# A megakernel on one core: FFN weights split in natural layout and turned by DMA, row terms joined behind the norm

## What is computed

```python
q1 = fake_quant(layernorm(x)); q2 = fake_quant(ctx)          # clip(round(x/s + z), 0, 255)
x = x + q1 @ q2
h = layernorm(x)
wg, wu, wd = block_qdq_weight(w_gate), ...                    # blocks of 32 along the input, 4 bits:
#   scale = max(|w|)/7 ;  wq = clip(round(w / scale), -8, 7) * scale
xq = act_qdq(h)                                               # 16 bits, one scale from min and max over all of h
up = act_qdq(xq @ wu.T); gate = act_qdq(xq @ wg.T)
gate = act_qdq(gate * fixed_qdq(sigmoid(gate)))
x = x + act_qdq(gate * up) @ wd.T
```

## Time and profile before

| | |
|---|---|
| median of three runs | 829.89 us |
| the profiled execution | 830.54 us |
| its span | 828.5 us |
| PE busy | 728.5 (88%) |
| DVE busy | 643.6 (78%) |
| ACT busy | 513.9 (62%) |
| POOL busy | 511.3 (62%) |
| mean granted TensorE clock | 0.954 |

### The profile page before, as it was taken

How to read it: one execution, slowest core, us unless ns; L and a number is a source line. 1 busy time by engine, 2 the same in 40 slices (tenths; PEclk the granted TensorE clock), 3 DMA queues, 4 the chain that set the end, 5 groups by cost and what they waited for, 6 DMA issues and landing times.

```text
span 828.5 us, 13514 instructions
## 1 busy us (share of the span) xinstructions
PE 728.5 (88%) x3443; PEld 342.7 (41%) x3443; DVE 643.6 (78%) x1374; ACT 513.9 (62%) x968; POOL 511.3 (62%) x488
## 2 busy tenths in 40 slices
PE   0688999736695996999999999999999788999998
PEld 0234545313232452444444444444444253444443
DVE  6885667678799678888888888888888767656655
ACT  4656766556857436777777777777776643655540
POOL 1986675546566557778888888888884414344330
PEclk9999999976888898999999999999999999999998
DMA  7211232201225326788666666666655512332311
GB/s 320 89 65 39 65 101 67 62 26 51 39 51 95 121 70 133 178 191 180 124 146 144 144 144 145 142 146 144 152 102 102 102 39 80 107 110 84 114 38 51
DMA packets 164500, 89.08 MB, mean 108 GB/s; under 512 B 154081, under 2 KB 154337, under 8 KB 161522
## 3 DMA queue, kind: packets, MB, share of 16 engines
q1 hardware_dynamic: 164466, 88.67, 42.9%
HBM read 49.85 MB, written 1.05 MB: 61 GB/s over the span
## 4 chain that ended last, share of the span: by engine, by line
PE 60%; DVE 13%; POOL 12%; issue 9%; DMA 2%; ACT 2%; SPq 1%; DVEq 0%; POOLq 0%; ACTq 0%
PE ps L950 19%; PE ps L951 19%; PE ps L952 19%; POOL arena L464 4%; POOL arena L472 3%; DVE arena L1290 3%; DVE arena L1293 2%; PE ps L1138 1%; POOL arena L604 1%; DMA arena<-arena 1%; DVE arena L1287 1%; POOL arena L451 1%; ACT arena L647 1%; POOL arena L482 1%; DVE ss L1449 1%
## 5 line engine op out<-in xcount | busy, mean ns | idle before, releaser
L950 PE MATMUL ps<-arena 128*128 128x512 f16 (+2 forms) x996 | 385.9, 388 | 25.7 <-DVE arena L1293 11.8
L951 PE MATMUL ps<-arena 128*128 128x512 f16 (+2 forms) x996 | 384.6, 386 | 0.0
L952 PE MATMUL ps<-arena 128*128 128x512 f16 (+2 forms) x996 | 384.2, 386 | 0.0
L647 ACT ACTIVATE arena<-arena 128x512 f16<-128x512 f32 (+9 forms) x392 | 260.8, 692 | 98.1 <-POOL arena L604 29.6
L1293 DVE SCALAR_TENSOR_TENSOR arena<-ps,arena 128x512 f32<-128x512 f32 (+2 forms) x182 | 122.9, 702 | 53.4 <-ACT arena L647 45.9
L950 PEld LDWEIGHTS ps<-arena 128*128 128x128 f16 (+1 forms) x996 | 99.5, 100 | 148.2 <-issue 34.6
L952 PEld LDWEIGHTS ps<-arena 128*128 128x128 f16 (+1 forms) x996 | 99.5, 100 | 122.6 <-issue 11.3
L951 PEld LDWEIGHTS ps<-arena 128*128 128x128 f16 (+1 forms) x996 | 99.5, 100 | 111.7 <-issue 9.2
L604 POOL TENSOR_SCALAR arena<-arena,rden 128x512 f32<-128x512 f32 x128 | 114.9, 898 | 25.3 <-DVE rden L1639 16.1
L1287 DVE TENSOR_TENSOR arena<-arena 128x512 f16<-128x512 f32 (+2 forms) x146 | 108.7, 779 | 5.3 <-ACT arena L647 4.8
L846 ACT ACTIVATE arena<-arena,mneg 128x512 f32<-128x512 f32 x124 | 88.5, 715 | 36.8 <-DVE mneg L1619 36.8
(11 more groups left out here) (126 smaller groups left out, 702.4 us busy)
## 6 DMA issues: line engine op xcount, KB each, us to landing
arena<-in_moe_w SPq DMA_DIRECT2D x18, 768.0 KB, 4.4
arena<-in_ffn_w SPq DMA_DIRECT2D x33, 256.0 KB, 2.7
arena<-in_wq SPq DMA_DIRECT2D x8, 1024.0 KB, 5.3
arena<-in_wo SPq DMA_DIRECT2D x8, 1024.0 KB, 5.3
arena<-in_kv_w SPq DMA_DIRECT2D x4, 1024.0 KB, 5.1
arena<-arena SPq DMA_TRANSPOSE x144, 3.3
arena<-in_ctx SPq DMA_DIRECT2D x1, 2048.0 KB, 9.5
arena<-in_ctx_t SPq DMA_DIRECT2D x1, 2048.0 KB, 13.9
```

The lines of the kernel that those rows point to most:

```text
L647: return a.activation(out_, in_, ACT.Copy, scale=scale, bias=bias)
L950: pe.matmul(out_, lhs[0], rhs[0], start=first, stop=False)
L951: pe.matmul(out_, lhs[0], rhs[1], start=False, stop=False)
L952: return pe.matmul(out_, lhs[1], rhs[0], start=False, stop=last)
```

## The change

It does four things.

1. The weights are no longer turned by PE. `scale_back` writes into one of four slots `deq`; ACT writes the high half from there (not from PSUM) and the low half is a subtraction of two SBUF tensors, on POOL for even chunks (`low`) and on DVE for odd ones (`weight_low`), both into `wt`, in natural layout. `turn_w(n)` on SP is a DMA transfer that transposes both halves (128x1024 f16) into `wfx`, where tile n reads them. `deq` and `wt` lie where `kt`, the turned K, comes later, so `turn_k(0)` waits until all turns have landed.
2. The chunks' parts run one or two chunks further ahead: ACT's high n + 2, POOL's low n + 2, scale_back n + 3, divide n + 4; DVE's maxima n + 5. All V units use banks 2 and 3. DVE's loops over chunks are unrolled.
3. In the first stage rounding is done by writing int32, which takes passes away: x from 3 to 2, ctx from 4 half passes to 2, the quantisation of `xn` from 3 flat passes to 2 for each row tile.
4. The row terms (`rsum`) are a constant for each row, which the norm removes, so the statistics no longer wait for them; ACT adds them after the extrema. The transposes of q1 are copied out earlier in ACT's order, `rstd(1)` stands between `kw_low(0, 1)` and `kw_low(0, 2)`, `spread(0)` after three V units and the transposes of the hidden after six.

```diff
+        wfx = carve(104, (WS, 2 * D), F16)
+        wf = [wfx[:, :, 0:D], wfx[:, :, D:2 * D]]
+        wt = carve(56, (DQ, 2 * D), F16)
+        deq = carve(64, (DQ, D))
...
+            def turn_w(n):
+                sp.wait_ge(w_lo[n % 2], n // 2 + 1)
+                if n >= WS:
+                    sp.wait_ge(f_ps, n - WS + 1)
+                sp.dma_start_transpose(wfx[:, n % WS].rearrange("p (a b) -> p a b", b=P),
+                                       wt[:, n % DQ]).then_inc(w_tr[n % DQ], 16)
...
+            for n in range(2, NCH):
+                turn_w(n)
+                if n + RAW + 1 < NCH:
+                    ring(n + RAW + 1)
+                if n == FT + 1:
+                    kw_load(3)
...
-                if n >= 2:
-                    g.wait_ge(w_t, n - 1)
-                g.tensor_tensor(deq[n % 2].rearrange("p (a b) -> p a b", b=QB), v, s, ALU.mult).then_inc(w_deq, 1)
+                if n >= DQ:
+                    g.wait_ge(w_lo[n % 2], (n - DQ) // 2 + 1)
+                g.tensor_tensor(deq[:, n % DQ].rearrange("p (a b) -> p a b", b=QB), v, s, ALU.mult).then_inc(w_deq, 1)
+
+            def low(n):
+                g.wait_ge(w_hi, n + 1)
+                g.tensor_tensor(wt[:, n % DQ, D:2 * D], deq[:, n % DQ], wt[:, n % DQ, 0:D], ALU.subtract)\
+                    .then_inc(w_lo[0], 1)
 
             def weights(n):
-                scale_back(n)
-                if n + 2 < NCH:
-                    divide(n + 2)
+                if n % 2 == 0 and n + 2 < NCH:
+                    low(n + 2)
+                if n + 3 < NCH:
+                    scale_back(n + 3)
+                if n + 4 < NCH:
+                    divide(n + 4)
...
-            for k in range(KD):
-                kw_low(0, k)
+            kw_low(0, 0)
+            kw_low(0, 1)
             rstd(1)
+            kw_low(0, 2)
+            kw_low(0, 3)
...
+            scale_back(0)
             kw_low(1, 2)
             kw_low(1, 3)
             v_low(3)
-            scale_back(0)
-            for u in range(4, MT - 1):
-                v_low(u)
-            g.wait_ge(xt_ps, KD)
             scale_back(1)
+            v_low(4)
+            v_low(5)
+            low(0)
+            v_low(6)
+            scale_back(2)
...
-                a.activation(half, half, ACT.Identity, bias=par[:, 3:4], scale=pc[:, 1:2]).then_inc(ctx_scaled, 1)
+                a.activation(ctx_int[:, b * KD:(b + 1) * KD], half, ACT.Relu, bias=par[:, 3:4],
+                             scale=pc[:, 1:2]).then_inc(ctx_scaled, 1)
...
-            a.wait_ge(row_terms, 1)
-            for t in range(NT):
-                a.wait_ge(col_added, t + 1)
+
+            def row_terms_in(t):
+
+                a.wait_ge(ext_ready, 1)
...
+            def weight_high(n):
+                a.wait_ge(w_deq, n + 1)
+                if n >= DQ:
+                    a.wait_ge(w_tr[n % DQ], 16 * (n // DQ))
+                copy(wt[:, n % DQ, 0:D], deq[:, n % DQ]).then_inc(w_hi, 1)
...
+            v_out(3)
+            for t in range(NT):
+                row_terms_in(t)
+            v_out(4)
+            weight_high(0)
+            v_out(5)
             hidden_high(0, 1.0)
+            weight_high(1)
+            v_out(6)
...
-                weight_high(n + 1)
+                weight_high(n + 2)
...
-                if i < FT - 1:
-                    weight_high(2 * FT + i + 1)
+                if i < FT - 2:
+                    weight_high(2 * FT + i + 2)
...
-                pe.wait_ge(w_lo, n + 1)
+                pe.wait_ge(w_tr[n % DQ], 16 * (n // DQ + 1))
...
-            for u in range(4):
+            for u in range(3):
                 v_unit(u)
             spread(0)
-            for u in range(4, MT - 1):
+            for u in range(3, 6):
                 v_unit(u)
             hidden_transposes(0)
-            v_unit(MT - 1)
-            pe.wait_ge(xt_lo, 1)
+            for u in range(6, MT):
+                v_unit(u)
             v_unit(MT)
...
-                stt(one(wf[1], n % WS), bank(2 + n % 2), SW, one(wf[0], n % WS), ALU.mult, ALU.subtract).then_inc(w_lo, 1)
+                tt(wt[:, n % DQ, D:2 * D], deq[:, n % DQ], wt[:, n % DQ, 0:D], ALU.subtract).then_inc(w_lo[1], 1)
...
-            own.link(ts(flat(xn), flat(xn), par[:, 2:3], ALU.add, MAGIC, ALU.add))
-            own.link(ts(flat(xn), flat(xn), MAGIC, ALU.max, MAGIC + 255.0, ALU.min))
-            ts(flat(q1), flat(xn), MAGIC + 128.0, ALU.subtract).then_inc(q1_ready, 1)
+            own.link(ts(flat(xn_int), flat(xn), par[:, 2:3], ALU.add, 0.0, ALU.max))
+            ts(flat(q1), flat(xn_int), 255.0, ALU.min, 128.0, ALU.subtract).then_inc(q1_ready, 1)
             for b in range(B):
-                half = flat(ctx_raw[:, b * KD:(b + 1) * KD])
                 v.wait_ge(ctx_scaled, b + 1)
-                own.mark(ts(half, half, MAGIC, ALU.add, MAGIC, ALU.max))
-            own.wait(own.n)
-            for b in range(B):
-                half = flat(ctx_raw[:, b * KD:(b + 1) * KD])
-                ts(flat(q2[:, b * KD:(b + 1) * KD]), half, MAGIC + 255.0, ALU.min, MAGIC + 128.0, ALU.subtract)\
-                    .then_inc(q2_ready, 1)
+                ts(flat(q2[:, b * KD:(b + 1) * KD]), flat(ctx_int[:, b * KD:(b + 1) * KD]), 255.0, ALU.min, 128.0,
+                   ALU.subtract).then_inc(q2_ready, 1)
...
-                v.wait_ge(row_added, t + 1)
+                v.wait_ge(col_added, t + 1)
...
-            own.link(ts(flat(xn), flat(xn), aqp[:, 0, 0:1], ALU.mult, MAGIC, ALU.add))
-            own.link(clip(flat(xn), 0))
-            ts(flat(xn), flat(xn), MAGIC, ALU.subtract, SINT, ALU.mult).then_inc(xn_ready, 1)
+            for t in range(NT):
+
+                own.link(ts(xn_int[:, t], xn[:, t], aqp[:, 0, 0:1], ALU.mult, aqp[:, 0, 2:3], ALU.min))
+                ts(xn[:, t], xn_int[:, t], SINT, ALU.mult).then_inc(xn_ready, 1)
...
-                m = block_maxima(n + 3)
-                weight_low(n)
-                m = scales(n + 3, m)
+                if n + 5 < NCH:
+                    m = block_maxima(n + 5)
+                if n % 2 and n + 2 < NCH:
+                    weight_low(n + 2)
+                if n + 5 < NCH:
+                    m = scales(n + 5, m)
                 if between:
                     between()
-                inverse_scales(n + 3, m)
+                if n + 5 < NCH:
+                    inverse_scales(n + 5, m)
```

More of the change, by code:

```diff
@@ L524, in _ @@
             divide(3)
-            weights(2)
+            weights(0)
             for k in range(KD):
@@ L558, in _ @@
                         k_low(u - 1)
-            for u in range(3, 2 * MT):
+            for u in range(4, 2 * MT):
                 k_pow(u)
@@ L1507, in _ @@
                 gate_front(i)
-            weights(2 * FT + 1)
+            for i in range(2):
+                weights(2 * FT + i)
             for i in range(2, FT):
```

152 lines of the change are left out of this document (62 added, 90 removed).

## The result

The changed kernel takes 833.49 us (median of five runs, 832.66 to 834.59) against 829.62 before in the same comparison: a ratio of 1.0054, 95% interval 1.003 to 1.0077. It is 0.5% slower, within the 1% that was called no change, and outside the 810 to 829 of the forecast. The profiled execution took 832.66 with a span of 830.8.

What follows compares the result with a forecast made beforehand. Bound by a cross-engine chain in the first stage, PE in the up tiles, the chunks' ring in late gate tiles, ACT and DVE in K. -18.3 to the third extrema, +7.5 in K: -10.8, so 819.5 us; range 810 to 829.

Steps and rivals of the forecast that it cites:

- the transfers' price: 33 new chunk transfers, each 3.1 to landing, hidden where PE sets the pace and costed at nothing.
- the ring of the last gate tiles: Last four gate tiles: a loop over ACT, POOL, DVE and PE, 5.9 per chunk before, is cut.
- the stall before `turn_k(0)`: K phase: ACT stands still while turn_k(0) waits for turn_w(32) to land; +7.5, bounds 0 and +9.
- Rival B: K phase: the stall at turn_k(0) is hidden or short; 812 us, 808 to 815; chance 0.20.
- D: DVE and POOL shut each other out of SBUF, the chunk's chain grows to 5.3; 845 us; chance 0.10.
- its eight passes of 0.54 end before 53.3: First stage: DVE's quantisation of the hidden per row tile starts at 48.0 and ends before 53.3.
- end by 43.4: First stage: PE's V0 to V2, at 2.6 each, end by 43.4, before the extrema are there.
- C: Gains lost in part, by the granted clock or a first stage still bound by POOL; 824 to 829; chance 0.20.
- what ACT has for it, 3.1 to 3.3: Gate tiles: a tile without V costs ACT's weight_high, rounding, copy and kw_high; five tiles taken at 3.3.
- 1.4 of loss until tile 5: Up tiles: tiles 2 and 4 wait for POOL's chunk parts; tile 5 at 82.8 against 90.83.
- I take 8.0: Up tiles: per pair PE 7.77, ACT 7.65, POOL 7.75; taken as 8.0, since they don't interlock exactly.
- I take no gain: K phase: ACT's wait on PE, 2.0 per pair, becomes a wait on DVE; no gain, bound -10.

Runs made afterwards that it cites:

- experiments 3 and 4: The changed kernel with the hidden quantised by two flat passes, 829.01 us; the changed kernel with POOL held until the hidden is quantised, 832.15 us (one run).
- experiment 6: The changed kernel with 40 added matmuls that keep PE busy ahead of V0; 831.3 us, ratio 1.0033 to the kernel before.
- experiment 7: The changed kernel with chunk 2's parts earlier in the orders of ACT and POOL; 831.8 us, ratio 1.0035 to the kernel before.
- experiment 5: The changed kernel with DVE's odd low halves one step later in the gating; 830.08 us, ratio 1.002 to the kernel before.

## Why the prediction was wrong

**What held.** The first extrema (44.5 forecast, 43.2), V0's start (35.6, 35.03), the transfers' price (3.1 to landing, 33 of them), the ring of the last gate tiles that is cut (5.9 apart before, 3.6 to 3.9 now), and the K phase: the stall before `turn_k(0)` was forecast with its place, its cause and 7.5 us, and it was 6.73 of wait; the stage is 7.3 longer. Rival B, that it would be hidden, is out. So is D at its price of 845, but not its mechanism: of the sixteen low halves on DVE five took 1.23 to 1.42, which was a sign of being wrong, and eleven 0.67 to 0.86.

The stages were forecast at 62.9, 44.0, 46.8 and 62.1 and took 67.9, 45.4, 52.0 and 62.0. Two terms failed, each by 5: the first stage and the gate tiles.

**The first stage, -9.4 forecast and -4.5 measured.** The step that failed most is the sentence "its eight passes of 0.54 end before 53.3". I had the rule of the ports in hand as rival D, with `rsum` as its row, and applied it only to the new subtractions, not to the eight short instructions that the same change makes of three long ones. They took 10.2 us instead of 4.3, as experiments 3 and 4 show. The right price was in the earlier trace rows: the flat pass took 1.96 beside POOL where the earlier trace rows has 1.22 for the form, 0.7 each; eight times that is the miss. Between V5's end and V6's start 4.9 passed instead of the 1.8 forecast; that is 3.1 of the 5.0 by which the first tile is late.

The other 2.0 are in V0 to V2, which should "end by 43.4" and ended at 45.7, behind the extrema. I used 2.6 per unit, the full-clock row, behind 10 us in which PE was idle; the drop of the clock stood among my rivals (C), but for the last gate tiles and not here. Worth 2.2 by the median of experiment 6.

**The gate tiles, 46.8 forecast and 52.0 measured.** I priced a tile without V by "what ACT has for it, 3.1 to 3.3" and left DVE out. The last ones came 3.6 to 3.9 apart, and DVE is busy 37.35 of the last 37.60 us; in 126 to 172 of the kernel before it was busy 32.81 of 46. Seven of its eleven 128x512 int32 passes in the changed kernel's gate stage took 1.14 to 1.30 instead of 0.53 (four took that long before), three of the six lows 1.23 or 1.24, and three of the scales of 128x16 0.89 to 1.01 instead of 0.17. So it was behind when the last tile was done, and the extrema took 7.6 from there instead of 4.7: 2.9 of the miss. The other 2.4 are ahead of it, at the seam between up and gate, where PE waited 1.32 and 1.21 for DVE and then ran the first half of tile 11 at half clock. That DVE sets this pace is read from the rows; no experiment took anything from it there.

**"1.4 of loss until tile 5."** From tile 0 to tile 5 it took 20.5; 18.4 before, 19.9 forecast. A small miss; experiment 7 takes 1.5 off this stretch.

**"I take 8.0" for a pair** of up tiles: the first took 7.8, the later ones 8.4 and 8.7, as before. In these PE waited 0.46 and 0.75 for a transfer, so the transfers, costed at nothing, were not wholly hidden.

**"I take no gain"** for what ACT no longer waits on PE in the K phase was right, and the wait on DVE that took its place was cheap to mend: 3.4 by experiment 5.

**What lies behind the change** was carried over unchanged. From the fifth extrema on it came out 1.7 longer in the profile, and from 3.1 shorter to 2.2 longer in the experiments, along with the granted clock.

Added up: the forecast was -18.3 to the third extrema, +7.5 in the K phase. Measured -6.7, +7.4 and +1.6. The loss was sized well; the gain in front of it was a third of what I took. Of the 7.4 by which the first extrema came earlier, 2.9 were gone by the first tile, on PE's clock and in DVE's short passes, and the gate stage gained 3.6 instead of 8.8.

## What to carry to other kernels

When a change cuts one long vector pass into many short ones beside a busy GpSimd, price them by the instruction and by rows in which both engines work, not by the element. When work is taken from the front of PE's queue, ask how long PE then stands idle: behind 10 us the next product ran at half clock in every trace here, and forty matmuls without use cost nothing there. When PE and ACT are relieved in a stage, add up every other engine's time for each tile with the other engine at work, since the pace may pass to one that had been idle. And a wait placed on a shared queue for the sake of one late user stalls all the earlier ones; give it only to the transfer that needs it.

## What the runs showed of the hardware

A 128x512 pass with one SBUF input (f32 to int32, int32 to f32) took 0.54 and 0.43 with GpSimd idle and 1.15 to 1.38 beside its products; a 128x2048 one took 1.29 with GpSimd idle (f32 to int32) and 1.9 to 2.1 beside them. A scale of 128x16 took 0.17 or up to 1.01. DVE's reductions of 128x512 took 0.67 all through the gate stage, with POOL busy 29.34 of 37.60 us. Forty added matmuls in 10 idle us kept the granted clock at 1.00 where it had been 0.61. Behind shorter waits the same code went either way: behind 1.93 us V6 ran at full clock in one trace and at half clock in four. And in three kernels that have the same code there, the last 27.8 us ran at a granted clock of 0.88, 0.92 and 1.00 in one profile each; the traces don't tell why.
